# Two linear products moved ahead of a round's attention in a pipelined transformer block

## The reference, cut to what matters

```python
x = x + tanh(g_xattn[0]) * shifted_memory(ctx, layernorm(x))      # "a": rows shifted by 19 or 77 tokens
x = x + tanh(g_ffn[0])   * quantised_linear(layernorm(x))         # "b": 512 -> 512, blocks of 32 quantised
x = x + tanh(g_xattn[1]) * attention(layernorm(x), ctx)           # "c", "d": Up = relu(. @ U), 77 keys, softmax, alpha @ ctx
x = x + tanh(g_ffn[1])   * switch_moe(layernorm(x))               # "e": top-1 router; then 8 experts 512 -> 2048 -> 512
```

## Time and profile before

| | us |
|---|---|
| median of 3 runs | 2079.48 (2077.41 to 2081.95) |
| the profiled execution, its own time | 2079.27 |
| its span in the profile | 2077.6 |
| PE busy | 1945.7 (94%) |
| DVE busy | 982.1 (47%) |
| POOL busy | 776.7 (37%) |
| ACT busy | 733.9 (35%) |

### The profile page before, as it was taken

How to read it: one execution, slowest core, us unless ns; L and a number is a source line. 1 busy time by engine, 2 the same in 40 slices (tenths; PEclk the granted TensorE clock), 3 DMA queues, 4 the chain that set the end, 5 groups by cost and what they waited for, 6 DMA issues and landing times.

```text
span 2077.6 us, 35395 instructions
## 1 busy us (share of the span) xinstructions
PE 1945.7 (94%) x11276; PEld 1681.7 (81%) x11277; DVE 982.1 (47%) x2270; ACT 733.9 (35%) x1691; POOL 776.7 (37%) x803
## 2 busy tenths in 40 slices
PE   4589999999999939999999999999999999999997
PEld 2568787787788728989889998999898898899986
DVE  3678999999998472333311142114224124112331
ACT  2235656656656442332411142114214114211231
POOL 0556576676674232342411142114305115211250
PEclk9589999999999959999999999999999999999999
DMA  6221343353343464341510043004305104300220
GB/s 198 98 88 43 138 174 120 130 172 117 138 163 102 162 209 123 97 142 42 168 42 30 30 143 94 30 30 141 108 16 180 36 30 154 95 30 30 75 87 11
DMA packets 152270, 208.81 MB, mean 101 GB/s; under 512 B 12830, under 2 KB 78622, under 8 KB 152197
## 3 DMA queue, kind: packets, MB, share of 16 engines
q1 hardware_dynamic: 111125, 114.14, 17.4%
q0 software_dynamic: 15728, 43.38, 6.9%
q10 hardware_dynamic: 25344, 50.33, 6.7%
HBM read 140.98 MB, written 68.37 MB: 101 GB/s over the span
## 4 chain that ended last, share of the span: by engine, by line
PE 82%; DVE 7%; issue 3%; DVEq 1%; ACT 1%; POOL 1%; POOLq 0%; ACTq 0%
PE bank L785 24%; PE bank L793 23%; PE bank L1469 9%; PE bank L1398 7%; PE bank L733 6%; PE bank L753 6%; PE bank L1450 2%; DVE x2T_lo L1788 1%; PE bank L711 1%; PE bank L742 1%; PE bank L1406 1%; DVE lg L1903 1%; DVE xdT_lo L1788 1%; DVE lb L1900 1%; DVE rd L1913 0%
## 5 line engine op out<-in xcount | busy, mean ns | idle before, releaser
L893 DVE SCALAR_TENSOR_TENSOR hT_lo<-bank,hT_hi 128x256 fp32r<-128x256 f32 x352 | 149.3, 424 | 671.4 <-ACT hT_hi L661 669.6
L661 ACT ACTIVATE hT_hi<-bank 128x256 fp32r<-128x256 f32 x352 | 135.1, 384 | 748.3 <-PE bank L785 733.5
L785 PE MATMUL bank<-inT_hi,w_lo 128*128 128x256 f32 x1408 | 398.5, 283 | 0.0
L785 PE MATMUL bank<-inT_lo,w_hi 128*128 128x256 f32 x1408 | 398.3, 283 | 0.0
L785 PE MATMUL bank<-inT_hi,w_hi 128*128 128x256 f32 x1408 | 396.9, 282 | 0.6 <-DVEq L941 0.6
L785 PEld LDWEIGHTS bank<-inT_hi,w_hi 128*128 128x128 f32 x1408 | 269.0, 191 | 14.3 <-DVEq L941 1.0
L793 PE MATMUL bank<-w_hi,hT_hi 128*128 128x512 f32 x704 | 279.9, 398 | 0.0
L785 PEld LDWEIGHTS bank<-inT_lo,w_hi 128*128 128x128 f32 x1408 | 269.0, 191 | 12.0
L793 PE MATMUL bank<-w_lo,hT_hi 128*128 128x512 f32 x704 | 277.7, 394 | 0.0
L793 PE MATMUL bank<-w_hi,hT_lo 128*128 128x512 f32 x704 | 274.1, 389 | 0.0
L785 PEld LDWEIGHTS bank<-inT_hi,w_lo 128*128 128x128 f32 x1408 | 269.0, 191 | 0.0
(11 more groups left out here) (312 smaller groups left out, 4019.2 us busy)
## 6 DMA issues: line engine op xcount, KB each, us to landing
stage<-in_L_ffn_W_dram SPq DMA_DIRECT2D x256, 256.0 KB, 3.1
X<-in_x_dram SPq DMA_DIRECT2D x16, 1024.0 KB, 5.3
t_d<-tt ACTq DMA_DIRECT2D x16, 1024.0 KB
x_d<-x ACTq DMA_DIRECT2D x16, 1024.0 KB
out_dram<-y ACTq DMA_DIRECT2D x16, 1024.0 KB, 8.4
xs<-in_x_dram SPq DMA_DIRECT2D x16, 768.0 KB
cw_a<-in_L_xattn_conv_w_dram SPq DMA_DIRECT2D x2, 1024.0 KB, 17.5
cw_b<-in_L_xattn_conv_w_dram SPq DMA_DIRECT2D x2, 1024.0 KB, 19.7
```

Source lines behind the costliest of these rows:

```text
L661: act.activation(hT_hi[:, f % 4, :], hb[f % 4][:, 0:CN], ACT.Relu).then_inc(e_hh, 1)
L785: last = pe.matmul(hb[f % 4][:, 0:CN], l[:, k, fs], r[:, k, :], start=(n == 0), stop=(n == 3 * KB - 1))
L893: dve.scalar_tensor_tensor(out=hT_lo[:, f % 4, :], in0=hb[f % 4][:, 0:CN], scalar=0.0, in1=hT_hi[:, f % 4, :].bitcast(F32), op0=ALU.max, o ...
```

## The change

On PE `linear(2)` is placed in front of alpha's turns, and `linear(3)` in front of `attend(0)`, so that `attend(0)` and `attend(1)` follow each other. DVE's and ACT's orders are altered with it. On DVE `scaled_logits` and `add_linear(2)` go in front of alT_lo, `positions` in front of `add_attention(0)`; `routed` stays behind it. On ACT the reciprocal root of b goes in front of alT_hi.

```diff
@@ ScalarE
                 if final(d):
                     chances()
+                if a is not None:
+                    rstd("b", a)
                 if d is not None:
                     wait(act, p_ca, d + 1)
                     wait(act, p_co, T * d)
                     wait(act, p_lb, d)
                     act.activation(alT_hi[:, :], b_s[0:L, :], ACT.Copy).then_inc(a_th, 1)
                 if a is not None:
-                    rstd("b", a)
                     wait(act, v_ln["b"], LN * (a + 1))
@@ TensorE
                 if draining:
                     project(0)
+                linear(2)
                 if d is not None:
                     for j in range(T):
                         wait(pe, a_al, T * d + j + 1)
                         last = pe.transpose(b_s[0:L, j * P:j * P + P], al[:, j, :], ident[:, :])
                     last.then_inc(p_ca, 1)
-                linear(2)
                 if draining:
                     project(1, logits)
+                linear(3)
                 attend(0)
-                linear(3)
                 attend(1)
@@ VectorE
                 add_linear(1)
                 if a is not None:
                     shift("b", a)
+                if not final(d):
+                    scaled_logits()
+                add_linear(2)
                 if d is not None:
                     wait(dve, a_th, d + 1)
                     dve.tensor_tensor(alT_lo[:, :], b_s[0:L, :], alT_hi[:, :].bitcast(F32), ALU.subtract).then_inc(v_tl, 1)
...
-                if not final(d):
-                    scaled_logits()
-                    if not final(e):
-                        scale_of_y()
+                if not final(d) and not final(e):
+                    scale_of_y()
+                if d is not None and not final(c) and not final(d):
+                    positions()
                 if final(c):
                     routed()
-                add_linear(2)
                 add_attention(0)
                 late_stats(0)
                 if final(e):
...
                 elif d is not None and not final(c) and not final(d):
-                    positions()
                     routed()
                 add_linear(3)
                 add_attention(1)
```

## The result

| | before | after |
|---|---|---|
| median of 4 runs, us | 2079.68 | 2095.33 (2094.05 to 2096.55) |
| the profiled execution, its own time | 2079.27 | 2095.76 |
| its span | 2077.6 | 2094.1 |
| mean granted clock of the span | 0.968 | 0.963 |

The ratio is 1.0072, 95% interval 1.0060 to 1.0084: slower by 15.65 us. Predicted were +6.7 and a range up to 2092. The sign was right, the size was less than half of it.

The account below looks back on a forecast made before the run. A closed loop of DVE and POOL, not PE, was taken to bound the rounds. Eleven rounds at 0.68 us make 7.5, less PE's 0.75 gives +6.7 on 2079.27: 2086.0; own range 2081 to 2092, drawn down to 2074 for nearby cases.

Parts of the forecast that it names:

- The bound: Token rounds: a closed loop of DVE and POOL, summing to 38.64 us, sets the 38.66 period; PE's loop has slack.
- The ends of the chain of moves: PE's moved products: linear(2) after add_linear(0) at 517.31, linear(3) at about 521.0, attend(0) at 523.86; PE gains 0.75 a round.
- The return in the router: DVE's lb, lg, rd end one POOL add earlier, rw is held to the fourth; net loss 0.68 us a round.
- PE's wait for al gone: Sign on PE: the wait at alpha's turns vanishes; one of some 2.5 us before linear(2) on DVE's X replaces it.
- no wait of DVE before up_lo: DVE's 0.67 us idle before up_lo vanishes, since PE is 0.75 earlier.
- Should the clock fall there in each round: Rival: in the gap before linear(2) the clock falls, 2.86 us more per linear product, 11 times, giving 2117; chance 0.04.
- DVE's wait before `add_attention(0)`: DVE idles 0.8 to 1.0 us for attend(0); rsum starts 1.08 later and flat 0.90 later.
- PE's gap: PE's spare time before linear(2) becomes one gap of about 2.7 us; the sign named some 2.5 us.
- The scatter: POOL's scatter, product, bias add and xs have no slack, so the next adds to X end 0.90 us later.
- PE's 0.75 in the round without z: In round 16 the loop is open, so PE keeps its gain of 0.75 us, subtracted from the sum.

Follow-up runs that it names:

- the gap filled: Changed kernel plus eight unused 512-column matmuls on PE before linear(2) in rounds 6 to 15; 2088.5 us, ratio 1.0046 to the kernel before.
- `routed` first: Changed kernel with routed() ahead of add_attention(0) on DVE and the router's exponentials moved ahead on ACT; 2096.0 us, ratio 1.0088 to the kernel before.
- `linear(3)` alone: Kernel before with only linear(3) moved in front of attend(0); 2098.5 us, ratio 1.0097.
- each filled kernel: Unused matmuls in PE's gaps, rounds 6 to 15; ratios to before: after 1.0046, linear(3) moved alone 1.0055, linear(2) moved alone 1.0081, after with routed first 1.0044.
- before, gaps joined: Kernel before, with the first of alpha's turns waiting for the last exponential, so PE's waits form one gap; 2085.1 us, ratio 1.0036.
- `linear(3)` alone filled: Kernel before with only linear(3) moved, plus 5 unused matmuls before alpha's turns in rounds 6 to 15; 2089.7 us, ratio 1.0055.

## Why the prediction was wrong in size

**Right.** *The bound.* The loop of DVE and POOL, not PE: PE took 5.1 us more work for nothing, and the period fell when DVE's part of the loop was shortened. *The ends of the chain of moves*, counted from `smx` (at 515.25 in the round of the earlier trace rows). `linear(2)` starts 2.2 behind `smx` (286.88 - 284.66; forecast 2.1, 517.31 - 515.25), `linear(3)` 5.8 (5.75), `attend(0)` 8.66 (8.61). *The return in the router*: rd at the third add, rw held to the fourth, 1.23 long. *PE's wait for al gone*, one before `linear(2)` in its place, and no wait of DVE before up_lo.

**The step that failed** is a rival that I had written down and put at 0.04: "Should the clock fall there in each round". It carries 9.6 to 9.9 of the 17.7 us. Against it stood only that the clock "stayed at 1.00 through 309 us with gaps of 2 us". There is no such gap in those 309 us (eight rounds, not nine). The pause before alpha's turns is 0.58 to 0.66 there and 0.96 once, then come three short ones within the turns, then 0.27. The one of 2.1 ends at 733.28, behind them, and there the clock is at half:

```profile
733.28 1.68 PE L1526 MATMUL bank<-ident,al 128*77 128x128 f32 x4 [2.14 <-ACT al L1269]
733.20:737.00 3.80, 1.68 (x4) 0.81 (x4) 2.48 (x12) 3.33 (x12) 3.02 (x4) 0.50 0.01 2
```

PE has little to do there, so this doesn't show that the pause lowered it; but the premise had no row, and the one row that bears on it points the other way. A single gap of 1.6 to 2.1 with nothing else changed lowers the clock in four rounds of nine, in the fastest of six executions. Its price was also off: the low clock lasted for part of a product, 1.35 a round in six rounds, not 2.86 in eleven.

**A term that was mis-sized.** DVE's wait before `add_attention(0)`: forecast 0.8 to 1.0, measured 1.46. I had let it start at the end of the third wide matmul; `attend` has two narrow ones behind it (ending at 294.30) and DVE starts 0.20 after these, 1.18 after the first wide one in place of my 0.89. So rsum came 1.39 later against `smx` (forecast 1.08) and `flat` 1.06 (297.11 - 284.66 = 12.45, before 11.39; forecast 0.90), some of it taken back since fewer instructions of `routed` were held. Hence 0.82 a round where 0.68 were forecast, and with less in the first two of the eleven rounds it makes 1.1 of the error (8.6 against 7.5).

**Not as forecast, small.** PE's gap: 2.0, not 2.5 to 2.7. The scatter has some slack, and DVE's q8 holds the link in its place. PE's 0.75 in the round without z was overlaid by slow matmuls, so that it can't be read off in after; with the gap filled the same round (t = 17) is not shorter either (37.29, before 36.28), with slow matmuls again, at 662.8 to 665.4. With `routed` first, where it has the full clock, it is 0.52 shorter.

**What stays open.** Why a gap lowers the clock in some rounds and not in others of the same kernel; its length alone doesn't tell (1.6 in nearly every round of `linear(3)` alone, 2.0 in six of nine of after). Nor is a gap the only thing ahead of a fall: in the round of t = 17 PE was busy through all of the 8 us before, and each filled kernel has one or two slow stretches in its ten filled rounds. What is shown is that the gap makes them frequent, and filling it makes them rare.

## What to carry to other kernels

An order that gathers an engine's small pauses into one is not neutral on TensorE: look in the stretches view for the granted clock behind the largest pause, and price that case at its full worth even where the present kernel shows 1.00. A product moved ahead of a short step delays that step by most of its length (`attend(0)` came 2.3 later for a product of 2.8); it is free only where nobody on the bounding loop waits for the short one. Before reordering, find the closed loop whose parts add up to the period and shorten that: here four small VectorE results in PSUM were worth more than any order tried. And a premise of the form "it stood this before" needs the row, with its place in time: here the long pause stood outside the stretch whose clock was quoted.

## What the runs showed of the hardware that was not expected

- A pause of 1.55 to 2.2 us between dense products was mostly followed by half clock, 0.3 to 2.2 us behind its end (1.0 to 1.4 in after): in four rounds of nine (before, gaps joined), six of nine (after) and nearly all of them (1.6, or 0.85 and 1.55 in one round). Of matmuls of 512 columns, six to eight then go by at 0.43 in place of 0.23 us.
- Eight matmuls without use, put into the pause, make the kernel 6.8 us faster (5.4 by the ratios).
- Not only instructions with two operands in SBUF are held by POOL: `over` and `pay`, TENSOR_SCALAR of 4 columns, took 0.50 and 0.48 in place of 0.17 and 0.23 under POOL's y (`routed` first against `linear(3)` alone filled and after).
